# One minimum for the decays' arguments, x times dt on GpSimd, and an output product moved ahead of the scores at a half's end

## What is computed

```
gate, xBC, dt = split(x @ in_proj_w.T)
x, B, C = silu(conv4(xBC) + conv_b)
dt      = softplus(dt + dt_bias)
cum     = cumsum(dt * A)                       # inside a chunk
Ldec    = tril(exp(cum[i] - cum[j]))
scores  = (C[i] . B[j]) * Ldec * dt[j]
y_intra = scores @ x
states  = sum_j dt[j] * exp(cum[last] - cum[j]) * B[j] x[j]
y       = y_intra + (C * exp(cum)) . state + D * x
g       = y * silu(gate)
out     = (g * rsqrt(mean over the group of g^2 + eps) * norm_w) @ out_w.T
```

## Time and profile before

| | us |
|---|---|
| median of 3 runs | 2126.28 (2123.61 to 2127.76) |
| the profiled execution's own time | 2117.76 |
| its span | 2115.8 |
| PE busy | 1973.0 (93%) |
| DVE busy | 1797.9 (85%) |
| ACT busy | 1447.2 (68%) |
| POOL busy | 1054.1 (50%) |

### The profile page before, as it was taken

How to read it: one execution, slowest core, us unless ns; L and a number is a source line. 1 busy time by engine, 2 the same in 40 slices (tenths; PEclk the granted TensorE clock), 3 DMA queues, 4 the chain that set the end, 5 groups by cost and what they waited for, 6 DMA issues and landing times.

```text
span 2115.8 us, 34810 instructions
## 1 busy us (share of the span) xinstructions
PE 1973.0 (93%) x11288; PEld 1528.3 (72%) x11288; DVE 1797.9 (85%) x4144; ACT 1447.2 (68%) x2756; POOL 1054.1 (50%) x1033
## 2 busy tenths in 40 slices
PE   8899896799999999999999999999999999999878
PEld 4666575587777777777777777777777777777655
DVE  5777674589899989998998999989999998999976
ACT  1566624577778777777787777777877777877621
POOL 4555240245555555546554645465546555654541
PEclk9999997899999999999999999999999999999989
DMA  4000010233222313232323232223232322222201
GB/s 169 2 0 0 1 56 19 85 110 110 71 79 96 124 65 106 76 115 66 109 86 104 86 89 95 86 85 89 96 98 72 108 92 90 81 90 80 96 19 40
DMA packets 125713, 166.09 MB, mean 79 GB/s; under 512 B 37777, under 2 KB 88977, under 8 KB 121330
## 3 DMA queue, kind: packets, MB, share of 16 engines
q1 hardware_dynamic: 125554, 164.11, 24.2%
HBM read 159.88 MB, written 4.20 MB: 78 GB/s over the span
## 4 chain that ended last, share of the span: by engine, by line
DVE 30%; PE 27%; ACT 21%; issue 7%; POOL 2%; SPq 0%; DMA 0%; ACTq 0%; POOLq 0%; DVEq 0%
DVE conv L807 10%; PE p_mix L102 6%; PE p_out L102 6%; DVE wq_t L1927 6%; PE p_gate_intra L102 5%; ACT wq_t L1780 4%; ACT L1790 3%; ACT L1780 3%; DVE w_out L1905 2%; PE p_gate_intra L1693 2%; DVE x_skip L1976 2%; ACT conv L785 2%; POOL wq_t L2156 2%; ACT x_and_gate L1790 2%; DVE p_gate_intra L1984 2%
## 5 line engine op out<-in xcount | busy, mean ns | idle before, releaser
L2156 POOL TENSOR_TENSOR wq_t<-wq_t,cb 128x1024 f32<-128x1024 f32 x128 | 309.3, 2416 | 386.0 <-ACT wq_t L1780 374.8
L102 PE MATMUL p_out<-w_out,yT 128*128 128x512 f32 x1536 | 383.7, 400 | 11.2 <-DVE yT L1937 11.2
L1927 DVE TENSOR_SCALAR wq_t<-cum_all,tables_in 128x128 f32<-128x128 f32 x1024 | 359.2, 422 | 4.1 <-DMA cum_all<-cum_rows 4.1
L807 DVE SCALAR_TENSOR_TENSOR conv<-p_mix,unit_small,conv 128x511 f32<-128x511 f32 (+2 forms) x384 | 287.0, 748 | 83.9 <-ACT conv L785 72.8
L102 PE MATMUL p_gate_intra<-x_high,w_gate 128*128 128x512 f32 x1024 | 351.5, 404 | 6.1 <-ACT x_and_gate L1790 4.9
L102 PE MATMUL p_mix<-x_high,w_x 128*128 128x512 f32 x1024 | 351.6, 405 | 1.4 <-DVE x_low L1155 1.4
L102 PEld LDWEIGHTS p_out<-w_out,yT 128*128 128x128 f32 x1536 | 290.7, 191 | 82.6 <-DVE yT L1937 15.0
L1780 ACT ACTIVATE wq_t<-wq_t,tables_in 128x128 f32<-128x128 f32 x1024 | 326.1, 390 | 4.9 <-DVE wq_t L1927 3.4
L795 ACT ACTIVATE x_and_gate<-conv 128x512 f32<-128x512 f32 x128 | 80.9, 632 | 259.4 <-DVE conv L807 259.2
L102 PEld LDWEIGHTS p_gate_intra<-x_high,w_gate 128*128 128x128 f32 x1024 | 194.3, 190 | 45.6 <-issue 6.1
L102 PEld LDWEIGHTS p_mix<-x_high,w_x 128*128 128x128 f32 x1024 | 193.7, 189 | 39.9 <-DVE x_low L1155 1.8
(11 more groups left out here) (242 smaller groups left out, 4216.7 us busy)
## 6 DMA issues: line engine op xcount, KB each, us to landing
cum_all<-cum_rows SPq DMA_DIRECT2D x128, 512.0 KB, 3.8
exp_cum<-exp_rows SPq DMA_DIRECT2D x192, 128.0 KB, 3.4
w_staged<-in_w_gate SPq DMA_DIRECT2D x16, 1024.0 KB, 5.5
w_raw_tiles<-in_w_x SPq DMA_DIRECT2D x64, 256.0 KB, 3.0
w_staged<-in_w_out SPq DMA_DIRECT2D x16, 1024.0 KB, 4.9
w_raw_tiles<-in_w_bc SPq DMA_DIRECT2D x16, 256.0 KB, 5.3
x<-in_x SPq DMA_DIRECT2D x1, 2048.0 KB, 18.6
out<-x_and_gate SPq DMA_DIRECT2D x8, 256.0 KB, 2.0
```

The source lines that it names most:

```text
L102: last = pe.matmul(dst, left[a](k), right[b](k), start=k == 0 and n_ == 0, stop=stop and k == tiles - 1 and n_ == 2)
L807: m = dve.scalar_tensor_tensor(self.conv[:, par, back:], self.p_mix[:, bank, 0:SEQ - back], w[:, TAPS - 1 - back:TAPS - back], self.conv[: ...
L1927: m = dve.tensor_scalar(decay[:, k % 2, h], cumB[:, h], own, own, ALU.min, ALU.subtract)
L2156: pool.tensor_tensor(decay[:, k % 2], decay[:, k % 2], cb[:, c].unsqueeze(1).to_broadcast([P, UNIT_HEADS, P]), ALU.mult).then_inc(decay_do ...
```

## The change

- `layer0_tail`: the logarithm of dt (ACT L1105, 128x1024), its small constant and PE's wait for it go. The second table holds dt itself.
- `arguments`: one DVE instruction, min of cumB and the head's own cum (spread over 128 tokens by a stride of zero), 128x1024, in place of eight 128x128 ones with two scalars each. The subtraction moves into the bias of ACT's exp, which is now minus own cum, from the new table `neg` (minus_cum).
- dt is multiplied into x: the new `to_scores` on POOL makes xdt = x_tokens * dt, 128x512, in every step, and PE's intra product reads xdt. `to_state` uses a new table `dtend` (group_dt_end, dt * exp(last - cum)).
- `end_logs` moves from DVE (k=15, and ahead of the mixer's first arguments) to POOL: at k=14 behind `decayed`, and ahead of the first low parts of w_gate at the mixer's start. It is one subtraction and one multiplication by -1, 128x128 each. `dt_end` is one POOL multiplication 128x128 at k=0 ahead of `decayed`. `inverse_rms` stands behind `to_scores`.
- xtok has one buffer. ACT fills it again once xdt of the step before is made.
- PE: at c = 7 the output product of the step before stands ahead of the wait for `decayed` and of the intra product, as in the other steps, not behind it.

```diff
-                    if i == CHUNKS:
-                        pe.wait_ge(soft, 6)
-                act.activation(log_dt[:], dt[:], ACT.Ln, bias=head_small[:, 3:4]).then_inc(soft, 1)
...
+        neg = n.sb("minus_cum", [P, 2, CHUNKS, 2 * UNIT_HEADS])
+        dtend = n.sb("group_dt_end", [P, CHUNKS, 2 * UNIT_HEADS])
+        xtok = n.sb("x_tokens", [P, UNIT_HEADS, HEAD_P])
+        xdt = n.sb("x_dt", [P, UNIT_HEADS, HEAD_P])
...
-                            if c < CHUNKS - 1:
-                                project_out(*before)
+                            project_out(*before)
...
                         pe.wait_ge(decay_done, s + 1)
-                        pe.wait_ge(flip_out, s + 1)
+                        pe.wait_ge(xdt_done, s + 1)
...
                         m.then_inc(intra_done, 1)
-                        if c == CHUNKS - 1:
-                            project_out(*before)
...
                     act.wait_ge(flip_done, step(g, k) + 1)
-                    wait(act, intra_done, step(g, k) - 1)
-                    wait(act, xs_done, n_feeds(g, k - 1) if k else n_feeds(g - 1, STEPS - 1))
+                    wait(act, xdt_done, step(g, k))
...
                         m = act.activation(decay[:, k % 2, h], decay[:, k % 2, h], ACT.Exp,
-                                           bias=tab[:, s // STEPS % 2, 1, c, head:head + 1])
+                                           bias=neg[:, s // STEPS % 2, c, head:head + 1])
...
                     wait(dve, intra_done, s - 1)
-                    for h in range(UNIT_HEADS):
-                        head = half * UNIT_HEADS + h
-                        own = tab[:, s // STEPS % 2, 0, c, head:head + 1]
-                        m = dve.tensor_scalar(decay[:, k % 2, h], cumB[:, h], own, own, ALU.min, ALU.subtract)
-                    m.then_inc(arg_done, 1)
+                    dve.tensor_tensor(decay[:, k % 2], cumB[:], over(tab[:, s // STEPS % 2, 0, c, mine], P),
+                                      ALU.min).then_inc(arg_done, 1)
...
+                    pool.tensor_tensor(logs[:], tab[:, g % 2, 2], tab[:, g % 2, 0], ALU.subtract).then_inc(logs_done, 1)
+                    pool.tensor_scalar(neg[:, g % 2], tab[:, g % 2, 0], -1.0, None, ALU.mult).then_inc(logs_done, 1)
...
+                    pool.tensor_tensor(dtend[:], tab[:, g % 2, 1], exps[:, 0], ALU.mult).then_inc(dtend_done, 1)
...
+                        def to_scores():
+                            wait(pool, intra_done, s)
+                            pool.tensor_tensor(xdt[:], xtok[:], over(tab[:, g % 2, 1, c, mine], HEAD_P),
+                                               ALU.mult).then_inc(xdt_done, 1)
+
+                        if k == 0:
+                            dt_end(g)
                         if c % CPS == 0:
-                            decayed()
+                            decayed(g, k)
+                        pool.wait_ge(flip_out, s + 1)
                         if feeds(c):
-                            pool.wait_ge(flip_out, s + 1)
                             to_state()
+                        to_scores()
+                        if not (first and k < 2) and older[1] >= CHUNKS:
+                            inverse_rms(*older)
                         if c % CPS:
-                            decayed()
+                            decayed(g, k)
+                        if k == STEPS - 2 and not last:
+                            end_logs(g + 1)
```

More of the change, by code:

```diff
@@ L938, in layer0_tail @@
         tables = n.sb("tables", [P, 2, CHUNKS, SSM_HEADS])
-        cumT, log_dtT = tables[:, 0], tables[:, 1]
-        log_dt = dt
+        cumT, dtT = tables[:, 0], tables[:, 1]
         pT = n.ps("pT2", [P, 2, 512])
@@ L1767, in group_exps @@
                     wait(act, state_steps, n_decays(g, 0))
-                    wait(act, xs_done, n_feeds(g, 0))
+                    wait(act, dtend_done, g)
                     act.activation(exps[:, 0].rearrange("p c h -> p (c h)"),
@@ L1906, in out_low_part @@
                                                  wo[:, 0, j].bitcast(F32), ALU.mult, ALU.subtract).then_inc(out_split, 1)
[L1908 to L1914 removed]
                 def arguments(s, k):
                     half, c = divmod(k, CHUNKS)
+                    mine = slice(half * UNIT_HEADS, (half + 1) * UNIT_HEADS)
                     dve.wait_ge(in_cum, s * 16 + 16)
@@ L2040, in group @@
                                         PLAN.ready(g, k - 1, ("x", UT - 1, c // CPS)))
+                            if not s:
+                                dve.wait_ge(in_tables, 80)
                             skip_part(g, k)
@@ L2043, in group @@
                             out_sum(g, c - 2)
-                        if k == STEPS - 1 and not last:
-                            end_logs(g + 1)
                         if half and c in (1, 2) and not last:
```

53 lines of the change are left out of this document (23 added, 30 removed).

## The result

The changed kernel is slightly slower, not faster. Over 20 runs of each, its median is 2128.64 us (2126.39 to 2132.81), that of the kernel before 2126.46 us (2122.28 to 2129.78); the ratio is 1.0015 with a 95% interval of 1.0008 to 1.0022. It is inside the range of 2103 to 2131 and inside the 0.2% called "same", but on the other side of no change than the forecast of 2119.3. A second measurement beside the last experiments gave 1.0006 (0.9991 to 1.0021). The profiled execution took 2127.0 us with a span of 2125.0.

A forecast was written before the change was run, and what follows sets the result against it. PE, busy 93% of the span, was taken to bound the groups. Groups 0, start -3.3 and last group -3.7 summed to -7.0 us: 2110.8 against the profiled execution, 2119.3 us against the median; range 2103 to 2131.

The forecast's parts named there:

- The arguments: DVE, every step: one minimum takes 1.25 us, saving 0.88 us a step undisturbed, hidden from PE in most steps.
- POOL's added work: x times dt, 1.05 us a step: 14 us more in a 220 us stretch with 99 us idle, so POOL doesn't become the bound.
- The swap: PE at k=7 and k=15: output product ahead of the intra product wins 0.3 us and 0.45 us a group.
- The half's starts: k=8 and k=0: x times dt on POOL delays DVE's weight splits, +0.9 us at k=8; +0.2 at k=0 after shorter arguments.
- The give-back of 0.4: Later waits, ACT's for y and those at k=4, 10 and 13, shrink with shorter arguments: -0.4 us a group.
- Sum of a group: One mixer group of 205.2 us: the terms sum to -0.05 us, taken as 0, ends -1.4 and +1.1.
- The start: Before the groups: -1.4 us where L1105 goes and -1.9 us in the mixer's first stretch, together -3.3 us.
- the tail: Layer 0's end, before the mixer: L1105 goes and the taps start right behind DVE's scans, -1.4 us.
- The last group: PE waits openly for DVE: -2.6 us at k=13 and again at k=14, +1.5 at k=12 and k=15 together; -3.7 us.
- C: Slower rival: every half's start pays 0.9 us, 15 times, and the swap returns nothing; 2132.8 us, chance 0.20.
- D: Rival: the swap removes all 29.9 us of PE's waits for the scores, nothing waits at p_out; -36.9, 2089.4 us, chance 0.08.
- A: The forecast itself: -7.0 us in sum, 2119.3 us with a spread of about 5, chance 0.48.

The follow-up runs named there:

- the eight minimums: The changed kernel with the swap undone, and eight 128x128 minimums with one scalar each in place of the one 128x1024: 2147.04 us, ratio 1.0088.
- The cut: The changed kernel with x times dt at c = 0 of each half cut to one head of eight, leaving work out: 2116.51 us, ratio 0.9955.
- the move to DVE: The changed kernel with the swap undone, and x times dt at c = 0 of each half on DVE instead of POOL: 2106.21 us, ratio 0.9899.
- the part of the product that fits: Swap undone, x times dt on DVE at half starts; now 3 (k=7) or 6 (k=15) of 12 output matmuls ahead of the scores: 2095.85 us.

## Why the prediction was wrong, point by point

The first profile of before was quick. The two first profiles are 9.2 us apart in span, the medians 2.2. Of the 9.2, 7.4 us arise in code that is the same in both, up to DVE's L1187 of before, which starts at 356.34 and whose counterpart starts at 363.71. Some 2 us arise in the first 14 us of the span, where the granted clock reads 1.00 in both and PE of the changed kernel waits once more for the first weights (1.31 us); the rest in half-clock stretches that only the changed kernel's trace has, 1.7 us at 44 to 48 and 3.7 us at 264 to 280 us. The prediction carried the profile's gap to the median over as a constant; this was no error of the sum, since the remainder, 9.2 - 7.4 = 1.8 us, is close to the measured 2.2.

Of the remaining steps, in the order of the prediction:

- **The arguments.** One minimum alone was put at 1.25 us and took 1.21 where nothing disturbed it (1232.14 in group 3). Its mean of 1.65 was inside "below 2.0". That nothing of it shows at the half's end was wrong: the scores of k=7 start 0.6 us sooner by it with the swap undone. The price of the form was mis-sized most: 0.88 us a step, called off the path in most steps, where the eight minimums beside x times dt cost 32 us in all, 8 of them as half clock. POOL's added work was mis-sized too: 16 steps of 1.05 us in 205 us are 18 us in the stretch of 220, not 14, and with the mean of 1.39 they are 24; POOL had room for either.
- **The swap, the step that failed.** The prediction gave it -0.3 us at k=7 and -0.45 at k=15, found against the scores' old start. At k=7 the two intervals together are 23.9 us in both kernels, less than 0.1 won. At k=15 nothing was won and 0.3 lost (14-15 and 15-0 are 27.8 against 27.5). It named the wait for the sum of halves that takes the idle time over, but the scores start 0.9 later, not 0.3: with the swap alone it is 0.4, and the other 0.5 comes with the two table instructions on POOL, which the prediction called hidden and put at 0. But it set the swap beside old arguments; with the new ones the gap at k=7 was 0.9 us, not 1.49, and the swap gave this gain away. Against the changed kernel without it, it costs 0.5 to 0.6 us at k=7 and 0.4 at k=15.
- **The half clock was not in the sum.** The idle time of 1.96 us now stands right ahead of twelve large matmuls, and 4 and 5 of 7 of them ran at half clock against 1 and 1 before: (4.5 - 1) x 1.57 = 5.5 us. In the kernel before, a like length of idle time (2.3 us) stood ahead of the scores.
- **The half's starts.** k=8-9 rose by 0.8 us where 0.9 was forecast. k=0-1 rose by 0.1 where 0.2 was. The cut and the move to DVE confirm the cause. The give-back of 0.4 came, 0.4 to 0.5, all at k=3-4.
- **Sum of a group.** -0.05 was forecast and 205.8 - 205.2 = +0.6 measured, before the half clock. Over eight groups this is 5 us, with the half clock 10.
- **The start.** -1.4 was forecast for the tail: from DVE's L1187 to the mixer's first instruction the changed kernel takes 1.8 us less (392.54 - 363.71 against 386.96 - 356.34). -1.9 was forecast for the mixer's start: to the mixer's first scores (416.32 and 419.53) it takes 2.4 less, with the 2.50 us wait gone. But PE's first gate product starts 2.3 us later in the mixer (4.35 for 2.05), not 0.6, since it waits 3.44 us for POOL's low parts, where before it waited 1.14: the term's two halves were both too small. Together -4.2 for -3.3.
- **The last group.** -3.7 was forecast. The waits of 3.67 us at k=13 and 14 became 0.83, and from the group's first scores to the end of the span 4.0 us are won.

```profile
2018.69 5.49 PE L102 MATMUL p_out<-w_out,yT 128*128 128x512 f32 x12 [0.83 <-DVE yT L1918]
```

These twelve matmuls take 5.49 us at half clock, for 4.35 in the row of before, but those of the next step take 4.78 for 5.49, so the clock gave little back here. The swap did: from the first scores to the last the group takes 185.9 us, and 183.9 with the swap undone, where the prediction had 1.5 for k=12 and k=15 together.
- **The rivals.** C had the mechanism (x times dt at the starts, and a swap that returns nothing) and the right sign, with 0.9 us a start where the cut found 0.75. D supposed that filling PE's wait is worth all 29.9 us; the part of the product that fits won 10.4 us on a kernel with 21.0 left. A's sign was wrong by the half clock and the swap's lost 0.6 us.

In sum: -4.2 at the start, +5 in the groups, +5 by the half clock, -4 at the end, +1.8. Start and end came within 1 us of the forecast; what failed is the groups' 0: the swap, which lost where it was to win 0.75 us a group, the table instructions put at 0, which by the timelines cost some 0.5 a group once the swap had taken the wait that hid them, and the half clock, for which the sum had nothing. Left open is why one idle time of 1.96 us is followed by half clock and the next, equal one isn't.

## What to carry to other kernels

In this kernel, filling a wait with other work of the waiting engine paid up to the length of the wait; what went beyond it delayed the released work and put idle time right ahead of a long row of matmuls, about half of which then ran at half clock. Put a piece of the work ahead, measured against the wait as the rest of the change leaves it, not as the old profile shows it. A wait also hides what comes late ahead of it, as the p_mix of k=15 here, and filling it brings that to light. When a change has several parts, run it without each: here one line cost more than the rest of the change gained.

## What the runs showed of the hardware

- PE idle for about 2 us, followed by the same twelve matmuls, ran at a granted clock of 0.50 (4.2 to 4.6 us) in 4, and in a second profile 5, of 7 otherwise equal groups, and at full clock (3.01 us) in the rest. Three more kernels with the full swap at k=15 had 2, 3 and 3 of 7. With 2.3 us of idle time and 16 short matmuls (1.09 us) ahead of the same twelve, it was 1 of 7 in each of two profiles, with 1.7 us 1 of 21 in the profiles of three kernels, with 2.0 to 2.1 us (the eight minimums) 5 of 15, and with gaps cut to 0.4 and 0.6 us none of 7. So the place of the idle time isn't the only thing that tells; what else does stays open.
- DVE's four weight splits with two operands in SBUF took 2.73 us where POOL's L2133 gave way to them, 3.70 beside x_to_state and the squares, and 4.47 beside x times dt as well; x times dt itself stretched from 1.05 us, its median, to a mean of 1.39 beside the long minimum, and to 1.10 beside the short ones. The same multiplication on DVE with one operand in PSUM took 692 ns in each of 16 places. This agrees with what the Trainium skill, page "SBUF — State Buffer", section "Who interferes with whom", says: a DVE instruction with two SBUF inputs contends with a GpSimd instruction that reads SBUF.
- A DVE cast with one input took 1.28 to 1.31 us in the seven places where POOL's `acc` ran beside it, and 0.42 us in the 57 others and in all 64 of the kernel before.
